# Batch 0's first row maxima from float32 row tiles, and an order of stages read from a table

## The reference

```python
# block 0: attention over all 1024 tokens of an image, 4 heads of 16 channels, then an MLP
qkv = einsum('bhwc,oc->bohw', layernorm(x, ln1_w, ln1_b), qkv_w)
attn = softmax(einsum('bhdn,bhdm->bhnm', q, k) / sqrt(16))       # 1024 x 1024 for each head
x = x + proj(einsum('bhnm,bhdm->bhdn', attn, v))
x = x + fc2(gelu(fc1(layernorm(x, ln2_w, ln2_b))))
# block 1: 8 heads of 64 channels; each token looks at itself and the 31 before it
t = t + window_attention(_ln_t(t), Wq, Wk, Wv, Wu, bu)
# block 2: batch norm of Wx over all batches, then yt = sigmoid(wx_t + yt @ V.T), 1024 steps
t = t + recurrence(_ln_t(t), W, V, gamma, beta)
```

## Time and profile before

| | before |
|---|---|
| median of the runs, us | 549.95 |
| lowest and highest of 3 | 546.73, 552.06 |
| span of the profiled execution, us | 543.8 |
| mean granted TensorE clock | 0.944 |
| TensorE busy | 463.1 us, 85% |
| VectorE busy | 327.1 us, 60% |
| ScalarE busy | 282.3 us, 52% |
| GpSimd busy | 11.0 us, 2% |

### The profile page before, as it was taken

One profiled execution on the slowest core, in us unless ns is written; L12 is line 12 of the kernel. 1 busy time (PEld: TensorE's weight loads), 2 busy tenths in 40 slices (PEclk: granted clock), 3 DMA queues, 4 the chain that ended last, 5 costly groups with the idle time before them and its releaser, 6 DMA issues.

```text
span 543.8 us, 7830 instructions
## 1 busy us (share of the span) xinstructions
PE 463.1 (85%) x3219; PEld 176.0 (32%) x3219; DVE 327.1 (60%) x604; ACT 282.3 (52%) x472; POOL 11.0 (2%) x14
## 2 busy tenths in 40 slices
PE   7768898988899898787899897899998988995884
PEld 2421222232233332232234332222333323542483
DVE  2569787789648653689468554696332545524414
ACT  2410476755773465564862563738864754172242
POOL 8000000000000000000000000000000000000000
PEclk9875699998999999999998999989999999997897
DMA  8685000007100000027000000000000000000003
GB/s 292 133 157 84 1 1 3 1 0 145 30 2 1 2 1 1 1 46 129 0 2 1 2 1 1 2 0 1 1 2 1 1 1 1 2 1 0 1 1 79
DMA packets 7476, 15.41 MB, mean 28 GB/s; under 512 B 1424, under 2 KB 4496, under 8 KB 7312
## 3 DMA queue, kind: packets, MB, share of 16 engines
q1 hardware_dynamic: 7440, 14.90, 12.5%
HBM read 10.61 MB, written 4.19 MB: 27 GB/s over the span
## 4 chain that ended last, share of the span: by engine, by line
PE 61%; DVE 22%; ACT 10%; DMA 3%; issue 2%; SPq 1%; DVEq 0%; ACTq 0%
DVE part_max L1083 9%; PE O L671 7%; PE R L719 5%; PE T L658 4%; PE T L638 4%; PE R L828 3%; PE R L658 3%; PE R L638 3%; PE R L597 3%; PE R L789 2%; PE R L605 2%; PE R L816 2%; PE R L803 2%; ACT rlog L985 2%; ACT probs L954 2%
## 5 line engine op out<-in xcount | busy, mean ns | idle before, releaser
L954 ACT ACTIVATE probs<-T 128x512 f32<-128x512 f32 x159 | 90.9, 596 | 81.4 <-PE T L658 80.9
L1083 DVE TENSOR_REDUCE part_max<-T 128x1 f32<-128x512 f32 x153 | 100.6, 683 | 36.6 <-PE T L638 36.5
L954 ACT ACTIVATE probs<-R 128x512 f32<-128x512 f32 x97 | 55.7, 596 | 46.8 <-PE R L658 46.5
L1083 DVE TENSOR_REDUCE part_max<-R 128x1 f32<-128x512 f32 x103 | 68.7, 683 | 9.8 <-PE R L638 9.7
L638 PE MATMUL T<-KX,QX 96*128 96x512 bf16 x153 | 63.4, 428 | 8.6 <-DMA KX<-qk_scratch 4.5
L671 PE MATMUL O<-probs,VT 128*32 128x512 f32 x512 | 67.7, 604 | 1.1 <-ACT probs L954 1.1
L658 PE MATMUL T<-QX,KX 99*128 99x512 bf16 x159 | 59.5, 393 | 3.5 <-DMA QX<-mx_part 2.6
L638 PE MATMUL R<-KX,QX 96*128 96x512 bf16 x103 | 42.5, 423 | 2.7 <-DVE part_max L1083 2.7
L658 PE MATMUL R<-QX,KX 99*128 99x512 bf16 x97 | 36.0, 388 | 1.4 <-DMA QX<-mx_part 1.2
L719 PE MATMUL R<-xp,abd 128*128 128x512 f32 x64 | 32.0, 603 | 1.2 <-DVE xp L1057 1.2
L638 PEld LDWEIGHTS T<-KX,QX 96*128 96x128 bf16 x153 | 15.0, 100 | 47.4 <-DVE part_max L1083 25.1
(11 more groups left out here) (210 smaller groups left out, 622.6 us busy)
## 6 DMA issues: line engine op xcount, KB each, us to landing
qk_scratch<-qk_part SPq DMA_DIRECT2D x8, 384.0 KB, 4.5
zs<-early SPq DMA_DIRECT2D x1, 2048.0 KB, 7.9
QX<-qk_scratch SPq DMA_DIRECT2D x4, 384.0 KB, 4.9
KX<-qk_scratch SPq DMA_DIRECT2D x4, 384.0 KB, 6.9
QX<-qk_scratch SPq DMA_DIRECT2D x4, 256.0 KB, 7.6
KX<-qk_scratch SPq DMA_DIRECT2D x4, 256.0 KB, 8.5
result<-probs SPq DMA_DIRECT2D x2, 512.0 KB, 5.2
s_rest<-rest SPq DMA_DIRECT2D x1, 882.0 KB, 10.2
```

The costliest lines, as they stand in the source:

```text
L954: A(probs[:, u % 2, h, :], ring["scores", b, u, h], ACT.Exp, scale=HD ** -0.5).then_inc(g["exp_done"], 1)
L1083: nc.vector.tensor_reduce(part_max[:, row, kh:kh + 1], ring["max_piece", b, half, i], AX_X, ALU.max).then_inc(g["max_red"], 1)
```

## The change

- **First maxima.** Batch 0, half 0, has no `max_piece` any more. Two more weights in the first pack (`wq_apart`, `wk_apart`, 256 columns) spread the four heads' 16 channels over partition groups of 32. `apart` projects half 0's queries and both halves' keys with them into T0 to T2; ScalarE copies them to `qk_apart` (in z's memory). `first_max(i)`, i from 0 to 7, makes for one query tile and one half of the keys four float32 matmuls, one per head, on 16 rows of its own 32-row group, each into its own bank: banks 0 to 3 for even i (O and T), 4 to 7 for odd i (R). One reduction on VectorE takes all four banks. `max_rows` of this half uses R0.
- **GpSimd splits batch 0.** The middle and low parts of batch 0 are made by GpSimd; `split(0)` is empty on VectorE. The relayout on SyncE still waits for `qk_lo`.
- **Head.** `products` stands behind `first_max(0)` and uses R2 and R3. Values of batch 0 are projected into bank O. Batch 1's layer norm and projection move out of the head, without their dummy matmuls (five and eight), and so do the four early maxima.
- **Places.** `attend_stages`, `merged`, `ROOM` and `COST` go. `lanes()` gives the scores and four lists (values, rest, last, maxima), and `PLACES` has a number for each stage of a list: it is put in front of the score with that number; numbers over 255 stand behind the last score. Batch 1's projection takes places 0 to 25, batch 2's 27 to 67, batch 3's 125 to 132. Batch 0's remaining stages take 70 to 124 (before, 74 to 128), batch 1's 133 to 212 (before, 138 to 192), batch 2's from 214 on (before, 194). Its block rounds stand behind the last score in both. Of the maxima, 75, 72, 58 and 19 stand in the four batches' scores, before 60, 64, 64 and 32.
- **Behind the last score.** `den(3)` follows `blk_out(2, 2)`; before, it followed `blk_den(2, 0)`.
- **Ring.** T0 to T2, R3 and R2 from the start.

```diff
-FIRST = {"mean_c": P, "vectors": len(VECTORS), "wq": P, "wk": P, "wv": P}
+FIRST = {"mean_c": P, "vectors": len(VECTORS), "wq": P, "wk": P, "wv": P, "wq_apart": P, "wk_apart": P}
...
+HEAD = [*layernorm_stages(0, 1), ("project", 0), ("split", 0), ("apart", 0), ("project_v", 0), ("first_max", 0), ("products",),
+        *(("first_max", i) for i in range(1, QT * 2)), *((n, 0, 0) for n in ("max_neg", "max_rows", "max_parts"))]
+def lanes():
+    scores = [("scores", b, u, h) for b in range(B) for u in range(UNITS) for h in range(H0)]
+    values = [("values", b, u) for b in range(B) for u in range(UNITS)]
+    maxima = [x for b in range(B) for half in range(2) if b or half for x in max_stages(b, half)]
+    rest = [*project_stages(1), *project_stages(2)]
+    for b in range(B - 1):
+        rest += [*mlp_stages(b), *layernorm_stages(b, 3), *window_stages(b), *out_stages(b, 0)]
+        if b == 0:
+            rest += project_stages(B - 1)
+    rest += [*window_stages(B - 1), *out_stages(B - 1, 1)]
+    last = [*mlp_stages(B - 1), *layernorm_stages(B - 1, 3)]
+    return scores, {"values": values, "rest": rest, "last": last, "maxima": maxima}
+PLACES = {
+    "values": [
+        6, 10, 14, 21, 23, 26, 32, 35, 38, 44, 48, 54, 54, 59, 62, 66, 72, 77, 79, 82, 85, 91, 93, 99, 104, 106, 108, 114, 119, 124, 127,
...
 def order_of_stages():
+    scores, others = lanes()
+    out, done = list(HEAD), dict.fromkeys(others, 0)
+    for at in range(max(max(PLACES[n]) for n in others) + 1):
+        for n, lane in others.items():
+            while done[n] < len(lane) and PLACES[n][done[n]] <= at:
+                out.append(lane[done[n]])
+                done[n] += 1
+        if at < len(scores):
+            out.append(scores[at])
+    return out
...
@@ gpsimd
+            pool.wait_ge(g["pool_fills"], 8)
+            for q in range(2):
+                pool.wait_ge(g["qk_rst"], q + 1)
+                nc.gpsimd.tensor_copy(mid_rows[:, q, :], qk_rest[:, q, :]).then_inc(g["qk_mid"], 1)
+            for q in range(2):
+                pool.wait_ge(g["qk_mid"], q + 1)
+                last = nc.gpsimd.tensor_tensor(qk_rows[:, 2 + q, :], qk_rest[:, q, :], mid_rows[:, q, :], ALU.subtract)
+            last.then_inc(g["qk_lo"], 1)
...
@@ tensor
+            def apart_(b):
+                for i, (w, half) in enumerate((("wq_apart", 0), ("wk_apart", 0), ("wk_apart", 1))):
+                    rows = half_rows(half)
+                    mm(T[:, i, :], t[w][rows, :], x_ln[rows, :], start=True, stop=True).then_inc(g["apart_mm"], 1)
+            def first_max(i):
+                nt, kh = divmod(i, 2)
+                if i == 0:
+                    pe.wait_ge(g["apart_in"], 3)
+                    pe.wait_ge(g["v_copied"], 1)
+                elif i == 1:
+                    pe.wait_ge(g["qk_rst"], 2)
+                    pe.wait_ge(g["abd_done"], 4)
+                else:
+                    pe.wait_ge(g["fmax_red"], i - 1)
+                for h in range(H0):
+                    rows = slice(h * HP, h * HP + HD)
+                    last = mm(banks8[:, i % 2 * 4 + h, :], qk_apart[rows, 0, nt * P:(nt + 1) * P], qk_apart[rows, 1 + kh, :], start=True, stop=True)
+                last.then_inc(g["fmax_mm"], 1)
...
@@ vector
             def split(b):
+                if b == 0:
+                    return
...
+            def first_max(i):
+                nt, kh = divmod(i, 2)
+                dve.wait_ge(g["fmax_mm"], i + 1)
+                rows = part_max[:, :, :].rearrange("p (h t) k -> p h t k", h=H0)[:, :, nt, kh]
+                nc.vector.tensor_reduce(rows, banks8[:, i % 2 * 4:i % 2 * 4 + 4, :], AX_X, ALU.max).then_inc(g["fmax_red"], 1)
```

More of the change, by code:

```diff
@@ L89, in project_stages, with max_stages @@
     return [*layernorm_stages(b, 1), ("project", b), ("split", b), ("project_v", b)]
[L92 to L97, removed]
+def max_stages(b, half):
+    return [("max_piece", b, half, i) for i in range(PIECES)] + [(n, b, half) for n in ("max_neg", "max_rows", "max_parts")]
 def mlp_stages(b):
     return [("den", b), ("den_exp", b), ("o_norm", b, 0), ("o_norm", b, 1), ("proj", b), *layernorm_stages(b, 2), ("fc1", b), ("fc2", b)]
[L105 to L119, removed]
-UNIFY_CUT = 3
[L123 to L127, removed]
+UNIFY_CUT = 3
 def unify_parts(b):
@@ L156, in window_stages @@
     if len(unify) > 1:
-        at = out.index(("blk_out", b, UNIFY_CUT)) + 1
-        first = unify[0] + out_stages(b, 0)
-        out[at:] = merged(out[at:], first)
+        out += unify[0] + out_stages(b, 0)
     return out + unify[-1]
[L163 to L184, removed]
@@ L188 @@
[L188 to L193, removed]
-def order_of_stages():
[L199 to L202, removed]
-        first = project_stages(b + 1) if 0 < b < B - 1 else []
-        other = rest_stages(b - 1) if b else []
-        start = FIRST_GAP * len(first)
-        if first:
-            main[:start] = [y for i, x in enumerate(main[:start])
-                            for y in ([x, first[i // FIRST_GAP]] if i % FIRST_GAP == FIRST_GAP - 1 else [x])]
-            start += len(first)
-        if b + 1 == B:
-            cut = other.index(("blk_scores", b - 1, LAST_CUT))
-            end = other.index(("ln_mean", b - 1, 4, 0))
-            other, late, norm = other[:cut], other[cut:end], other[end:end + 4]
-        out += merged(main, other, start)
-    early = mlp_stages(B - 1)
-    out += merged(late, early)
-    for x, y in zip(norm, layernorm_stages(B - 1, 3)):
-        out += [x, y]
-    return out + [("wx", B - 2, 0), *window_stages(B - 1), *out_stages(B - 1, 1)]
@@ new lines @@
+PLACES = {
+    "values": [
+        6, 10, 14, 21, 23, 26, 32, 35, 38, 44, 48, 54, 54, 59, 62, 66, 72, 77, 79, 82, 85, 91, 93, 99, 104, 106, 108, 114, 119, 124, 127,
+        131, 136, 139, 144, 146, 150, 155, 157, 164, 171, 175, 175, 182, 185, 188, 192, 195, 201, 202, 207, 211, 216, 219, 222, 227, 230,
+        236, 239, 244, 246, 253, 256, 257,
+    ],
+    "rest": [
[11 rows of a table added]
+    ],
+    "last": [
+        263, 267, 269, 270, 272, 273, 274, 276, 276, 277, 277, 277, 278, 278, 278,
+    ],
+    "maxima": [
[9 rows of a table added]
+    ],
+}
@@ L936, in project, with apart_ @@
                     A(hi_rows[:, q, :], R[:, q, :], ACT.Copy).then_inc(g["qk_hi"], 1)
+            def apart_(b):
+                for i in range(3):
+                    act.wait_ge(g["apart_mm"], i + 1)
+                    A(qk_apart[:, i, :], T[:, i, :], ACT.Copy).then_inc(g["apart_in"], 1)
             def project_v(b):
@@ L1345 @@
     arr["wq"], arr["wk"], arr["wv"] = both(turned[0].T), both(turned[1].T), both(wqkv[2 * C:].T)
+    for i, n in enumerate(("wq_apart", "wk_apart")):
+        w = np.zeros((C, H0, HP), f)
+        w[:, :, :HD] = wqkv[i * C:(i + 1) * C].reshape(H0, HD, C).transpose(2, 0, 1)
+        arr[n] = twice(w.reshape(C, P))
     wp = np.zeros((P, C), f)
```

91 lines of the change are left out of this document (39 added, 52 removed), and 20 rows, old and new, of the table PLACES.

## The result

The changed kernel takes **521.65 us** (median of four runs, 517.16 to 523.77), the kernel before 548.34 beside it: a ratio of 0.951, interval 0.944 to 0.958. The forecast was 527 (507 to 547), faster. The total was met to 1%; two of its terms were not.

A forecast was written before the change was run, and what follows sets the result against it. The head waits for a scratch read and 32 maxima; in the stream TensorE is busy 317 of 354 us. Span 543.8 - 14.2 (head) - 4.7 (stream) - 6 (waits) + 2 (tail) = 520.9; with 6.15 more, 527 us (507 to 547).

The forecast's parts named there:

- Head: Up to the first score: early maxima without the scratch bring it to 45.3 instead of 59.45, -14.2 us.
- The tiles themselves are worth nothing in the sum: Head: 1.0 us of matmul against 2.2 of reduction per step, so only the early start gains.
- The rival: Head: row tiles run one after another at 3.6 us a step, total 540 us; chance 0.08.
- GpSimd: Head: its split of batch 0 takes 2 us, at four times the rate 8, and stays hidden.
- Moved work: Batch 1's projection and four early maxima join batch 0's scores: 5.3 us of TensorE and 7.8 of VectorE.
- At the same ratio 349.1: -4.7 us: Stream: busiest engines' sums fall from 295.9 to 291.8 us; times the old 1.196, 349.1 instead of 353.8.
- the waits of maxima: Stream: separate places for maxima cut TensorE's waits behind VectorE; -6 us, nothing to -20 possible.
- The fourth rival: Places work better than credited: stream at ratio 1.10, 321 us, tail 0, total 503 us; chance 0.15.
- The tail: Behind the last score: batch 3's denominator starts about 8 us later, fewer rounds woven in after; +2, bounds -4 and +12.
- queries of batch 3 within 49 us of the last score: Sign for the tail: batch 3's queries come at most 49 us after the last score.
- Relayout of batch 1: Batch 0's scores: issued near 56, lands 17 us later, just before its first maximum; costed at nothing, perhaps a few us.
- 6.15: Whole kernel: us by which the median of the runs lies above the profiled span, added to 520.9 for 527.

The follow-up runs named there:

- e8: Changed kernel with the four matmuls of each first-maxima step all reading head 0's 16 rows; 560.01 us, ratio to before 1.019.
- e2: Changed kernel with the second step of the first maxima also waiting for batch 0's rows to return from DRAM; 540.99 us, ratio to before 0.984.
- e4: Changed kernel with VectorE instead of GpSimd splitting batch 0; 525.25 us (516.34 to 527.36).
- e1: New head of the changed kernel, with the order behind it made by the old rules, no table of places; median 555.0 us, ratio to before 1.008.
- e5: Changed kernel with each batch's stages of `rest` at even distances inside the batch; 624.72 us, ratio to before 1.140.
- e6: Changed kernel with each half batch's maxima at even distances; 560.07 us, ratio to before 1.020.
- e10: Changed kernel with the values at their old places, one after every fourth score; 555.50 us, ratio to before 1.012.
- e12: e1 with `rest` divided among the batches as in the table, spread by the old rules inside each; 562.86 us, ratio to before 1.029.
- e11: Changed kernel with the projections of batches 1 and 3 up to 3 scores earlier; 524.30 us, ratio to before 0.954.

## Why the prediction was right, and where not

- **Head: right.** -13.6 for -14.2. The first projection (12.7 for 12.6), the end of step 0 (22.0 for 22.2), the reduction (2.24 us apart for 2.2) and the path behind the last (5.6 for 5.5) came within 0.2; step 7 ended at 40.3 for 39.8. The bounds on the reduction alone, 44.6 to 46.7, held the first score.
- **"The tiles themselves are worth nothing in the sum": too strong.** It held only because they run side by side; e8 shows 37 us without that. The rival was priced at 3.6 us a step and 540 us, the full clock's price; at the half clock that the head had from its second half on, a step took 6.7 and the total was 560. The Trainium skill (TensorEngine Tiling (Array Packing), Performance Considerations) says that PSUM's emptying may become the bound behind fast tiles; the trace agrees, narrowly at the half clock: 2.15 us of matmul against 2.24 of reduction.
- **GpSimd: hidden, as said, and for nothing.** 3.7 us from 15.34 to 19.05, where the fill rows gave 2 with 8 as the end; the rows were back at 38.5 (e2), inside the 35 to 41; the two differences took 2.27 us, VectorE's 1.29. By the Trainium skill (GPSIMD Engine Reference, Performance versus the Vector engine) about twice was to be expected; here 1.76 times. By e4 VectorE hides them as well.
- **Moved work: right.** Batch 0's term in the sums, 10.5 us at the ratio 1.196, is 12.6; measured 13.1, and 13.2 in e1. But it stood inside the net of -4.7: the text has "batch 0 longer by some 10 us" among its signs and never sets it against the head's gain, which it eats whole.
- **Stream: the step that failed.** "At the same ratio 349.1: -4.7 us", and 6 for the waits of maxima: -10.7 in all; measured -20.6. The ratio of time to the busiest engines' sums was taken as a constant of the kernel, when it is what the places change: 333.2 / 291.8 = 1.142. e5, e6 and e10 refute the step itself: with the table's work in each batch, and so the same 291.8, their streams took 439, 376 and 361 us, ratios of 1.50, 1.29 and 1.24. e12, with `rest` divided by the table under the old rules, took 382. The fourth rival had the direction (1.10); its 503 took the stream 12 us too short and the tail at 0.
- **The tail: a term mis-sized.** +2 with bounds -4 and +12; measured +11.3, of which 7.0 are idle time, the order's, and 4.3 the same work at a lower granted clock (0.91 for 0.94), which no run shows to be the order's. The later start of 8 us was seen (11.1 measured); "fewer rounds woven into it after" was credited with 6 us that were not there, since the rounds' waits for the logarithm had lost the MLP work that covered some of them. The sign "queries of batch 3 within 49 us of the last score" failed: 54.4.
- **Relayout of batch 1: as warned.** 17.2 us to landing for 17; the wait of 2.6 is one of the "few us" that it might become.

The span came out at the 520.9 us of the sum because the stream's extra 9.9 us paid for the tail's extra 9.3 and the head's missing 0.6; that is luck. So is part of the distance to 527: the median lies 0.75 above the span, where 6.15 had been added. Each run on record lies 1.7 to 2.0 us above its own span; the rest of the 6.15 came from a profiled execution of the kernel before that was some 4 us shorter than its median run. It stays open why so small a shift as e10's costs as much as e6's: the waits are many and short, and no single chain was followed.

## What to carry over

An early start that works by pushing other work behind it gains only where that work finds idle time; do the head alone once to see it. Sums of engine time by batch say what a stretch can't beat, not what it takes: with engines that run in order, the same stages took from 333 to 439 us of stream by their places alone. Measure even small moves: up to 4 scores on 49 of the values cost 34 us (e10), up to 3 on the 12 stages of two projections nothing clear (e11). Look at TensorE's idle time and at the granted clock in each stretch, since the same matmuls took 7.5 us more behind the last score in e1 than in the kernel before at the same idle time. Keep independent work between the steps of any chain that is left bare at the end.

## What the runs showed of the hardware

- In e8 TensorE was busy for 48.6 of 52.9 us with 16-row matmuls, and the granted clock was 0.50, its lower level, throughout.
- In the changed kernel one VectorE reduction takes 2048 columns over four PSUM banks in 2.29 us; the 512-column form takes 0.683 us (mean of 153).
- The Trainium skill (TensorE: Matmul & The Clock Gate, Part 3) gives 3.07 times for four row tiles of 32 rows and 512 columns; with 16 rows each, the runs here show 3.1.
